# The order of TensorE's three products in unpacking 4-bit weights, with separate releases for the two banks that they fill

## The reference, cut to what matters

```python
wq = qw[:, None, :] >> shifts[None, :, None] & NIB
wq = wq.reshape(-1, qw.shape[1]).astype(jnp.float32)
zq = (qz nibbles) + 1.0
return sc[g_idx] * (wq - zq[g_idx])
...
w_gu = dequant(qweight_gu, qzeros_gu, scales_gu, g_idx_gu)      # 512 x 2752
gate, up = (inter[..., :INTER], inter[..., INTER:])             # INTER = 1376
h = silu(gate) * up
w_d = dequant(qweight_down, qzeros_down, scales_down, g_idx_down)  # 1376 x 512
out = x + h @ w_d
```

## Time and profile before

| what | value |
|---|---|
| median of 3 runs | 871.94 us (868.27 to 872.51) |
| the profiled execution: its own time | 870.51 us |
| the profiled execution: its span | 868.8 us |
| mean granted clock of TensorE | 0.933 |
| PE busy | 792.7 us, 91% of the span |
| DVE, ACT, POOL busy | 56%, 49%, 34% of the span |
| span of the unpacking on DVE | 45.9 to 141.1 us |

### The profile page before, as it was taken

How to read it: one execution, slowest core, us unless ns; L and a number is a source line. 1 busy time by engine, 2 the same in 40 slices (tenths; PEclk the granted TensorE clock), 3 DMA queues, 4 the chain that set the end, 5 groups by cost and what they waited for, 6 DMA issues and landing times.

```text
span 868.8 us, 24146 instructions
## 1 busy us (share of the span) xinstructions
PE 792.7 (91%) x10116; PEld 565.1 (65%) x10119; DVE 488.0 (56%) x1000; ACT 427.9 (49%) x817; POOL 297.3 (34%) x297
## 2 busy tenths in 40 slices
PE   5455778899999999999999999999999999999898
PEld 5411324465788578857885787578767876786484
DVE  9978663543656465746564656466646654554321
ACT  1656665452655265526652665266526662565120
POOL 2155455232145214521453144304430543054020
PEclk9655665999999999999999999999999999999899
DMA  8943223000010101011001100120011000100000
GB/s 276 264 119 88 59 73 85 26 3 2 26 29 3 50 27 29 3 51 35 21 3 49 46 9 3 51 53 2 3 49 53 2 3 25 29 3 14 13 2 24
DMA packets 21512, 37.04 MB, mean 43 GB/s; under 512 B 4158, under 2 KB 8414, under 8 KB 21404
## 3 DMA queue, kind: packets, MB, share of 16 engines
q1 hardware_dynamic: 21404, 35.48, 14.1%
HBM read 26.47 MB, written 4.19 MB: 35 GB/s over the span
## 4 chain that ended last, share of the span: by engine, by line
PE 70%; DVE 14%; issue 7%; ACT 7%; POOL 1%; DVEq 0%; ACTq 0%; POOLq 0%
PE bank L556 17%; PE bank L571 13%; PE bank L527 10%; PE bank L537 9%; PE bank L697 4%; PE bank L714 3%; DVE nmf L1275 3%; PE bank L583 3%; PE bank L690 3%; ACT arena L918 3%; PE bank L504 2%; PE bank L671 2%; DVE stats L1212 1%; DVE arena L1207 1%; DVE small L1060 1%
## 5 line engine op out<-in xcount | busy, mean ns | idle before, releaser
L556 PE MATMUL bank<-arena,WGU 128*128 128x256 f16 (+1 forms) x2112 | 248.4, 275 | 1.4 <-DVE arena L762 1.4
L556 PEld LDWEIGHTS bank<-arena,WGU 128*128 128x128 f16 (+1 forms) x2112 | 206.9, 101 | 28.1 <-DVE arena L762 1.7
L1463 POOL TENSOR_TENSOR arena<-arena 128x512 f16<-128x512 f32 x128 | 147.0, 1177 | 207.2 <-ACT arena L925 207.2
L571 PE MATMUL bank<-WD,arena 128*128 128x512 f16 (+1 forms) x528 | 121.0, 379 | 0.0
L918 ACT ACTIVATE arena<-bank,small 128x512 f32<-128x512 f32 x128 | 89.2, 776 | 54.9 <-PE bank L697 54.9
L1453 POOL TENSOR_TENSOR arena<-arena 128x512 f16<-128x512 f32 (+1 forms) x48 | 51.8, 1078 | 172.2 <-ACT arena L901 172.2
L527 PE MATMUL bank<-arena,WT 128*128 128x256 f16 x768 | 90.9, 281 | 2.9 <-DVE arena L762 2.5
L527 PEld LDWEIGHTS bank<-arena,WT 128*128 128x128 f16 x768 | 77.1, 101 | 16.3 <-issue 4.2
L537 PE MATMUL bank<-WT,arena 128*128 128x512 f16 x384 | 86.8, 383 | 0.0
L571 PEld LDWEIGHTS bank<-WD,arena 128*128 128x128 f16 (+1 forms) x528 | 49.3, 97 | 53.3
L1275 DVE TENSOR_REDUCE nmf<-bank 128x8 f32<-128x512 f32 x128 | 79.3, 681 | 5.6 <-PE bank L671 5.4
(11 more groups left out here) (172 smaller groups left out, 1002.2 us busy)
## 6 DMA issues: line engine op xcount, KB each, us to landing
arena<-in_L_ffn_qweight_gu SPq DMA_DIRECT2D x8, 688.0 KB, 5.5
arena<-arena SPq DMA_DIRECT2D x32, 144.0 KB, 2.7
WT<-in_ctx SPq DMA_DIRECT2D x8, 512.0 KB, 9.7
arena<-in_ctx SPq DMA_DIRECT2D x8, 512.0 KB, 3.7
arena<-in_x SPq DMA_DIRECT2D x8, 512.0 KB, 3.9
out_y<-arena SPq DMA_DIRECT2D x16, 256.0 KB, 2.0
arena<-in_L_ffn_qweight_down SPq DMA_DIRECT2D x10, 256.0 KB, 3.5
arena<-in_L_xattn_Wk SPq DMA_DIRECT2D x1, 1024.0 KB, 5.8
```

Source lines behind the costliest of these rows:

```text
L556: mm = e.matmul(pb[0:m, i * TOK:(i + 1) * TOK], WGU[:, sp, kb, half * INTER + fb * P:half * INTER + fb * P + m], x2T[:, mp, kb, :], start= ...
L571: mm = e.matmul(pb[:, :], hT[0:m, sp, fb, t * P:(t + 1) * P], WD[0:m, mp, fb, :], start=(n == 0), stop=(n == 3 * FB - 1))
L1463: e.tensor_tensor(phl[:, a, 1, :], pring[:, a, :], phl[:, a, 0, :], ALU.subtract).then_inc(S["p_lo"], 1)
```

## The change

In `pe_dequant` the two products that form the difference now come first. They wait only until the scaled copy of unit n-2 has been taken (`d_scaled`), which is the last reader of the bank `diff`. The gathering of the scales comes behind them, waits until the multiplication of unit n-2 is done (`d_w`), the last reader of the bank `scale`, and sets a new semaphore `d_scale`. DVE's multiplication waits for `d_scale` as well as for `d_scaled`. In ACT's tick the scaled copy of unit n-2 now stands ahead of the conversion of unit n.

```diff
@@ pe_dequant
-            reached(e, S["d_w"], n - 1)
-            e.matmul(scale[0:m, 0:cols], hot[0:64 + groups, pick], sc3[0:64 + groups, c0:c0 + cols], start=True, stop=True)
+            reached(e, S["d_scaled"], n - 1)
             e.matmul(diff[0:m, 0:cols], hot[0:groups, pick], z[0:groups, c0:c0 + cols], start=True, stop=False)
             e.wait_ge(S[f"d_conv{n % 2}"], n // 2 + 1)
             e.matmul(diff[0:m, 0:cols], ident16[0:m, 0:m], wbf[n % 2][0:m, 0:cols], start=False, stop=True).then_inc(S["d_gathered"], 1)
+            reached(e, S["d_w"], n - 1)
+            e.matmul(scale[0:m, 0:cols], hot[0:64 + groups, pick], sc3[0:64 + groups, c0:c0 + cols],
+                     start=True, stop=True).then_inc(S["d_scale"], 1)
@@ act_ticks
             for n in ticks(place):
+                act_dequant_scaled(e, n - 2)
                 if n % 2:
                     dequant_conv(lambda out, src: e.activation(out, src, ACT.Copy), e, n)
-                act_dequant_scaled(e, n - 2)
                 act_dequant_hi(e, n - 4)
@@ dve_dequant_w
             e.wait_ge(S["d_scaled"], n + 1)
+            e.wait_ge(S["d_scale"], n + 1)
             e.tensor_tensor(w, w, dq_banks(n)[1][0:m, 0:cols], ALU.mult).then_inc(S["d_w"], 1)
```

More of the change, by code:

```diff
@@ L274, in build @@
             "sc_high", "sc_rest", "hot_ready", "hotd_ready", "zd_ready",
-            "d_int", "d_conv0", "d_conv1", "d_gathered", "d_scaled", "d_w", "d_hi", "d_lo",
+            "d_int", "d_conv0", "d_conv1", "d_gathered", "d_scale", "d_scaled", "d_w", "d_hi", "d_lo",
             "x_loaded", "ctx_loaded", "v_stacked", "y_stored0", "y_stored1",
```

## The result

The changed kernel takes 860.78 us (median of 4 runs, 860.50 to 860.94), the kernel before 870.11 us in the same comparison: a ratio of 0.9894 with a 95% interval of 0.987 to 0.9918, so 1.1% faster. A second comparison gave 860.63 us and 0.9884 (0.9867 to 0.9901). The forecast was 862.5 us in a range of 858.5 to 869.0. The profiled execution has a span of 858.9 us, 9.9 less than before.

What follows compares the result with a forecast made beforehand. A chain of waits in the weight unpacking was taken as the bound, POOL next; gains 4.15 + 2.65 + 1.95 = 8.75 us gave 861.8 from the profiled execution, 863.2 from the median, so 862.5, range 858.5 to 869.0.

Steps and rivals of the forecast that it cites:

- the ring of 3.76 us: Weight unpacking: TensorE, ACT and DVE wait on each other in a circle, 3.76 us per pair of full units.
- Rival 1: Unpacking: POOL's instructions and DVE's shifts exclude each other, 3.83 us a pair, 869 us in all; chance 0.14.
- w0: Unpacking place of 9.08 us before: last multiplication done earlier, 1.2 us won here, 1.65 in all by then.
- w1: Unpacking place up to the key projection: that starts at 83.4 to 83.6, about 4.15 us won in all.
- the filling in "scales": First unpacking place, pipeline only filling: multiplications of units 1 and 2 come 0.5 earlier, 0.45 us won.
- values: Last unpacking place: three pairs of 3.2 instead of 3.76 us and no waiting tick at the end, 1.95 us won.
- keys: Unpacking place of 16.25 us: five pairs with POOL full throughout, 2.65 us won.
- nothing there is touched: After the first chunk TensorE is busy without a break, so the change acts only in the unpacking, 45.9 to 141.1 us.
- The new wait on DVE: DVE's multiplication also waits for the gathering of scales; covered by the scaled copy with 0.4 us to spare, cost nothing.
- Rival 2: Unpacking: ACT's queue and POOL run in turn, 4.46 us a pair, 878 us in all; chance 0.06.
- rival 3: Unpacking: more waits in TensorE's order than seen, 3.45 us a pair, half the gain, 866.5 us; chance 0.18.
- rival 4: The change does nothing because another chain of chunk 0 ends last in each place, 871 us; chance 0.04.

Runs made afterwards that it cites:

- short low parts on POOL: The kernel before, with POOL copying where it should subtract for the low parts, output wrong: 870.10 us, ratio 0.9987.
- TensorE's part: The whole change without the swap on ACT, so TensorE's new order and separate releases alone, against the kernel before: 858.56 us, ratio 0.986.
- ACT's part: The kernel before with only the scaled copy moved ahead of the conversion on ACT: 864.71 us, ratio 0.9929.
- the second profile: The whole change measured and profiled again, on another chip, against the kernel before: 860.63 us, ratio 0.9884.
- short low parts behind the change: The whole change, with POOL copying where it should subtract for the low parts, output wrong: 854.07 us, ratio 0.9812 against the kernel before.
- one release: The whole change, but all three TensorE products wait for the multiplication of unit n-2: 864.10 us, ratio 0.9912 against the kernel before.
- the one with TensorE kept busy: The whole change without the swap on ACT, plus five extra products ahead of chunk 0's query projection: 859.19 us, ratio 0.9869 against the kernel before.

## Why the prediction was right

**The bound of before.** Right. It was the ring of 3.76 us through L488, L491, the conversion, the copy and the multiplication: short low parts on POOL left it at 3.76, and each of three ways to cut it shortened it: both parts to 3.14, TensorE's part to 3.14, ACT's part to 3.48.

**The next bound.** Right. The forecast was 3.2 us for a pair with POOL full, measured 3.14, with no idle time between POOL's instructions, and 2.98 when its low parts were short, where I had put TensorE's bound at 2.94 to 3.0. What is not shown is that POOL stands alone: with fewer conversions on POOL and more on ACT the time stayed. Rival 1, full exclusion of POOL and DVE's shifts with 3.83 a pair, is ruled out for this mix. DVE's full-width shifts took 0.65 us on the mean, as before (0.64), with single ones up to 1.41. At one place that I had not looked at, the table below, a step of DVE did take twice its time beside POOL. There the rule of the Trainium skill (SBUF — State Buffer, "SBUF: two separate sides"), that GpSimd and a VectorE operation in a two-port mode block each other for a whole instruction, fits the row: L1168 starts 0.98 us before POOL's low parts end and takes 1.71, its 0.87 and most of those 0.98. Whether L1168 runs in such a mode no run here shows.

**The waits that take the old one's place.** I named the right one, that the scaled copy waits for POOL's low part with the conversion behind it in ACT's queue, and called it balanced with nothing to spare. In the steady pair that is so: 3.14 us with the swap and without it. At the entries it is not: the swap costs some 2 us in U, 0.5 each in "w0" and "w1", because the conversion stands behind a copy that waits for POOL and comes 1.5 us later for it. The step that failed is that I priced this wait in the steady ring alone. The working had the copy of unit 5 waiting until 59.95, 2.35 us after DVE's entry (measured 2.58), and took the conversion behind it as given.

**What the unpacking gives.** 6.7 us (7.1 by the second profile) where the sum said 8.75. Nearly all that is missing lies ahead of the key projection: 2.3 us were won there where 4.15 were forecast. "w1" gave 2.1 of 2.5, and two terms were mis-sized outside the places. The table between "w0" and "w1" was costed at nothing and took 0.5 more: with the faster "w0" POOL's last two low parts now lie beside it, and one step of it is held up. Before, that step was alone:

```profile
68.56 0.87 DVE L1166 TENSOR_SCALAR WD<-WD 96x1376 f32<-96x1376 f32 x1
```

In the changed kernel it reads as follows, beside POOL's row:

```profile
66.58 2.73 POOL L1435 TENSOR_TENSOR WGU<-arena,WGU 128x352 f16<-128x352 f32 x2
68.33 1.71 DVE L1168 TENSOR_SCALAR WD<-WD 96x1376 f32<-96x1376 f32 x1
```

The same two low parts took 2.08 us before. With short low parts behind the change the gap between "w0" and "w1" was 0.8 us shorter. The other is the filling in "scales", forecast at 0.45 and measured at -0.3; POOL's first conversion came 0.55 later after the first shift in this execution. In the second profile it came 0.09 later and the filling won 0.14, so the 0.45 was in neither, and the rest varies from one execution to the next. "values" gave 2.1 where 1.95 was forecast, "w0", "w1" and "keys" each 0.2 to 0.4 less than forecast.

**What lies behind the unpacking.** The forecast counted nothing there but 0.9 either way for the projections. It gave 4.0 us, of which the query projection is 1.0. That the total came out near the forecast is thus partly chance: 2 us too much in one term, 4 us missing in another, and a setup that ended 0.8 later. The step that failed is "nothing there is touched": no instruction was, but the clock that TensorE is granted in chunk 0 and in the last chunk was another. That the change causes this is not shown: it held in both its profiles and not in the one of the kernel before, and the runs of the swap alone fall on both sides.

**The new wait on DVE** was costed at nothing: DVE waited for L492 three times, 2.0 us in all and 0.9 at most, and how much of that lies on the path was not tried. **Rival 2** (ACT and POOL in turn) is refuted by the row of POOL without idle time, **rival 3** by the pair of 3.14, **rival 4** by the result.

## What to carry to other kernels

Cutting a ring brings the time down only to the next full engine, so work out each engine's time for one period before and after; here that gave 3.2 where 3.14 was measured. Do not put an instruction whose inputs are ready behind one that waits for the engine that is about to become the bound: price such a wait at the entry of a stage, where queues have run dry, and not in the steady period alone. And look at the gaps between the stages: moving a table to where its engine was idle and a high part ahead of the stage gave 4.9 us more, on top of the better half of the change.

## What the runs showed of the hardware

- A part of the program that was not touched can differ by 4 us, 0.5% here, along with TensorE's clock. From the query projection to the end the profiled executions took 720.4 to 721.6 us or 724.1 to 724.9 us and nothing between. All of the second group (the kernel before, the swap alone, one release, short low parts before the change) have the stretch at the lower clock in the attention of chunk 0; of the first group only the one with TensorE kept busy has it, and made it up in the query projection. Within one kernel time follows the mean clock too: the 14 runs of the kernel before in one comparison have 867.74 us at 0.938 and 873.13 at 0.933. And one kernel can be on either side: the swap alone took 868.4 and 868.7 us at 0.935 in two runs and 862.6 to 866.3 at 0.936 to 0.940 in eight. No run of the kernel before had more than 0.938, and none of the whole change less than 0.940.
- More work on TensorE ahead of a dense stretch raised the clock within it sooner (5.73 us against 7.37 for 48 products), and in the same execution a stretch at the lower level later on took the gain back. What decides whether that stretch appears is not settled: nothing was run that changed it alone.
- A VectorE step of 0.87 us took 1.71 beside POOL's low parts, while a pair of low parts there took 2.73, which had taken 2.08 without the table beside it. The two hold each other up, and by the pair of 3.14 by far less than in full where steps are short.
